# Routing a mixture of experts on one core: the outputs of 20 tiles go through memory and come back as one row per token

## The reference

```python
gates = sinkhorn(gate_logits)                    # 8 iterations; [b, token, expert], 8 experts
g = jnp.swapaxes(gates, -1, -2)
gv, idx = jax.lax.top_k(g, m)                    # each expert takes m = 64 of 512 tokens
hard_gates = (gate_values > 0.5).astype(x.dtype)
routed = xh[bi, hi, routed_indices]
out = jnp.einsum('bhmei,ehio->bhmeo', routed, experts4)
out = out * hard_gates[..., None]
y = jnp.zeros_like(xh).at[bi, hi, routed_indices].set(out)   # the last write of a token wins
x = x + y
```

## Time and profile before

| | |
|---|---|
| median of 3 runs | 493.18 us (491.93 to 494.08) |
| profiled execution, its own time | 492.21 us |
| span of its profile | 490.5 us |
| busy share of the span | PE 85%, DVE 82%, ACT 63%, POOL 47% |
| attention and its preparation | 0 to about 375 us |
| Sinkhorn | to 418.4 us |
| top 64 | 418.4 to 436.2 us |
| ranks | 437.3 to 449.3 us |
| weights and bits | 449.3 to 453.5 us |
| selection | 453.5 to 487.8 us |
| last output DMA | 487.8 to 490.5 us |

### The profile page before, as it was taken

How to read it: one execution, slowest core, us unless ns; L and a number is a source line. 1 busy time by engine, 2 the same in 40 slices (tenths; PEclk the granted TensorE clock), 3 DMA queues, 4 the chain that set the end, 5 groups by cost and what they waited for, 6 DMA issues and landing times.

```text
span 490.5 us, 9349 instructions
## 1 busy us (share of the span) xinstructions
PE 418.8 (85%) x2827; PEld 209.1 (43%) x2827; DVE 404.0 (82%) x1616; ACT 308.9 (63%) x599; POOL 228.1 (47%) x411
## 2 busy tenths in 40 slices
PE   5448987998999999899999989999988965999563
PEld 4233444464545546344554644555444432434121
DVE  6968756898898789788878978887986876996997
ACT  1002684788678769867876986887777432543871
POOL 3142573567466356746635674543433210000895
PEclk9955988999999999999999999999999999999998
DMA  8770143035027004402701440270001010100122
GB/s 261 213 174 2 49 135 76 34 115 113 21 78 182 25 33 131 99 20 77 182 25 45 126 110 2 97 162 24 2 1 64 2 43 0 43 23 21 43 65 86
DMA packets 28434, 36.85 MB, mean 75 GB/s; under 512 B 2144, under 2 KB 24224, under 8 KB 26912
## 3 DMA queue, kind: packets, MB, share of 16 engines
q1 hardware_dynamic: 27312, 34.68, 25.4%
q10 hardware_dynamic: 1072, 1.57, 1.3%
HBM read 19.41 MB, written 16.78 MB: 74 GB/s over the span
## 4 chain that ended last, share of the span: by engine, by line
PE 53%; DVE 23%; ACT 8%; issue 7%; DMA 5%; POOL 1%; SPq 1%; POOLq 1%; DVEq 1%; ACTq 0%
PE PVB L494 11%; PE ROWB L469 10%; PE CHB L482 9%; PE MB L526 6%; PE MB L502 4%; PE MB L536 4%; ACT YS L736 4%; DVE JUNK L938 3%; DMA YS<-parts_scratch 3%; PE ROWB L628 3%; DVE YS L1229 2%; PE CHB L628 2%; DVE CHB L1229 2%; PE MB L515 2%; DVE X L1235 2%
## 5 line engine op out<-in xcount | busy, mean ns | idle before, releaser
L938 DVE CUSTOM_DVE_ANT_0 JUNK<-ROWB,TRI 128x384 bf16<-128x384 f32 (+3 forms) x512 | 221.7, 485 | 41.7 <-PE ROWB L469 38.2
L736 ACT ACTIVATE YS<-CHB 128x512 f32<-128x512 f32 x320 | 172.9, 612 | 44.0 <-PE CHB L482 43.7
L858 POOL TENSOR_SCALAR_AFFINE_SELECT YS<-YS 128x256 f32<-128x256 f32 x256 | 102.4, 410 | 147.2 <-ACT YS L736 139.4
L469 PE MATMUL ROWB<-YS 96*128 96x384 bf16 (+3 forms) x512 | 122.2, 312 | 13.1 <-DVE MX L938 7.1
L482 PE MATMUL CHB<-YS 104*128 104x384 bf16 (+3 forms) x512 | 116.4, 303 | 7.4 <-ACT YS L736 5.0
L494 PE MATMUL PVB<-YS,VP 128*32 128x512 f32 (+3 forms) x1024 | 95.2, 446 | 5.1 <-POOL YS L858 5.1
L469 PEld LDWEIGHTS ROWB<-YS 96*128 96x128 bf16 x512 | 43.8, 100 | 89.9 <-DVE MX L938 47.1
L696 ACT ACTIVATE YS<-MB 8x1024 bf16<-8x1024 bf16 x32 | 32.5, 1017 | 57.4 <-PE MB L515 57.4
L482 PEld LDWEIGHTS CHB<-YS 104*128 104x128 bf16 x512 | 46.0, 98 | 41.7 <-ACT YS L736 17.6
L494 PEld LDWEIGHTS PVB<-YS,VP 128*32 128x32 f32 x1024 | 35.1, 109 | 31.7 <-POOL YS L858 17.5
L938 DVE DVE_READ_ACCUMULATOR2_ANT MX<- 128x1 f32 x512 | 42.2, 82 | 0.0
(11 more groups left out here) (131 smaller groups left out, 520.0 us busy)
## 6 DMA issues: line engine op xcount, KB each, us to landing
YS<-parts_scratch SPq DMA_DIRECT2D x28, 384.0 KB, 6.7
parts_scratch<-PARTS SPq DMA_DIRECT2D x15, 384.0 KB, 2.4
parts_scratch<-PARTS SPq DMA_DIRECT2D x15, 256.0 KB, 2.1
X<-in_x SPq DMA_DIRECT2D x8, 256.0 KB, 5.4
xn_scratch<-XN2S SPq DMA_DIRECT2D x8, 256.0 KB, 2.0
XS<-xn_scratch SPq DMA_DIRECT2D x8, 256.0 KB, 2.6
out<-X SPq DMA_DIRECT2D x8, 256.0 KB, 2.3
parts_scratch<-PARTS SPq DMA_DIRECT2D x15, 128.0 KB, 1.7
```

The lines of the kernel that those rows point to most:

```text
L469: last = pe.matmul(ROWP[BANK[u]][:, col:col + keys], QP[par][0:ROWS_K, pair, P * qb:keys], KZ[par][i % 2][0:ROWS_K, pair, 0:keys], start=T ...
L736: act.activation(PT[s % 2][:, c, :], CH[BANK[c]], ACT.Exp).then_inc(exp_done, 1)
L858: pool.affine_select(out=v, in_=v, pattern=[[0, 2], [1, P]], compare_op=ALU.is_ge, fill=0.0, base=0, channel_multiplier=-1).then_inc(causa ...
L938: last = dve.tensor_tensor_reduce(out=JUNK[BANK[u]][:, col:col + n], in0=ROWP[BANK[u]][:, col:col + n], in1=TRI[:, T - n:T], scale=1.0, sc ...
```

## The change

- The outputs of tiles 0 to 19 still go to `YS`, and SP stores each from there to a memory tensor `expert_outputs` (512 KB a tile; one row of 128 values for each token and expert, row 0 all zeros). The loads of `XS` for batches 2 to 6 stand between these stores in SP's program.
- ACT's scaling, POOL's sums and the DVE steps on stored tiles are gone. DVE works out a row number for each token of the 20 tiles (`IDX`, 0 if the token gets nothing). POOL then issues 20 indirect DMAs; each reads one row for each of 128 tokens and adds it to `X`.
- DVE selects only tiles 20 to 31, in six pairs, both of a pair from PSUM. A fourth bank pair (`ROWP[2]`, `MB`) is added; PE's tile 24 and later wait for the pair before last.
- Ranks: for each pair of lists PE now makes four small products, with 128 columns of `OH` as the weights and two columns of `RANKC` moving. They land with tokens on partitions, so the copy to `RT` and the four transposes go. The half tiles stand after pairs 6, 12, 18 and 24.
- The first round of the top 64 reads PSUM; the copy to `GT` goes. So does the copy of `BITS` to PSUM.
- The outputs of batches 5 to 7 are issued by ACT, those of 0 to 4 by SP.
- `SMALL` grows by 160 columns (80 KB); POOL clears one more row (`NOTHING`) at the start.

The diff, without declarations and without the host's table:

```diff
@@ -127,28 +127,20 @@
 DIRECT = 5
 STORED = DIRECT * TB
-SHARE = [[2, 3]] * DIRECT
-OTHERS = [[t for t in range(TB) if t not in own] for own in SHARE]
+ROWS_AT = T + 2 * B * E - 2 + E
-OWN = [(b, t) for b in range(DIRECT) for t in SHARE[b]]
-PAIRED = [((n // TB, n % TB), OWN[n - STORED]) for n in range(STORED, B * TB - 2)] + \
-         [((B - 1, TB - 2), (B - 1, TB - 1))]
+PAIRED = [((n // TB, n % TB), ((n + 1) // TB, (n + 1) % TB)) for n in range(STORED, B * TB, 2)]
 SELECT_STEPS = 4
 def selected_by(b):
     return 2 * SELECT_STEPS * (1 + max(k for k, pair in enumerate(PAIRED) if any(of == b for of, _ in pair)))
-def folded_by(b):
-    return 4 * sum(map(len, OTHERS[:b + 1]))
 class Batch:
...
@@ -274,10 +264,11 @@
         SUMS = (ROWP[2], MB)
         FIRSTB = ROWP + CH[0:2]
         EXPB = [CHB[:, 0:2 * T], ROWB[:, 0:2 * T]]
-        DIRECTB = [(CH[0], CH[1]), (ROWP[0], ROWP[1]), (CH[2], PVB[:, :])]
-        BITP = ROWP[2][:, 0:3 * B * TB].rearrange("p (k n) -> p k n", k=3)
+        DIRECTB = [(CH[0], CH[1]), (ROWP[0], ROWP[1]), (CH[2], PVB[:, :]), (ROWP[2], MB[:, :])]
+        y_dram = nc.dram_tensor("expert_outputs", [1 + STORED * P * E, C], F32, kind="Internal").ap()
         xn2_dram = nc.dram_tensor("xn2_scratch", [B, P, T], F32, kind="Internal").ap()
         scratch = nc.dram_tensor("parts_scratch", [2, 2, PRODUCTS, HD, 2, PAIRS, T], BF16, kind="Internal").ap()
...
@@ -432,15 +413,19 @@
             load_xn2(0)
             load_xn2(1)
             save_xn2(B - 1)
-            for b in range(2, B):
+            sp.dma_start(y_dram[0:1, :], NOTHING[:, :]).then_inc(y_saved, 16)
+            for n in range(STORED):
+                sp.wait_ge(y_copied, n + 1)
+                sp.dma_start(y_dram[1 + P * E * n:1 + P * E * (n + 1), :].rearrange("(p e) c -> p (e c)", e=E),
+                             YS[:, C * E * n:C * E * n + C * E]).then_inc(y_saved, 16)
+                if n % TB == TB - 1:
+                    load_xn2(n // TB + 2)
+            for b in range(DIRECT + 2, B):
                 sp.wait_ge(y_full, TB * (b - 1))
-                if b == B - 1:
-                    sp.wait_ge(xn2_saved, 16 * B)
+                sp.wait_ge(xn2_saved, 16 * B)
                 load_xn2(b)
-            for b in sorted(range(B), key=lambda b: (selected_by(b), -b)):
-                sp.wait_ge(chain, selected_by(b))
-                if b < DIRECT:
-                    sp.wait_ge(folded, folded_by(b))
+            for b in range(DIRECT):
+                sp.wait_ge(gathered[b], 16 * TB)
                 sp.dma_start(out[b].rearrange("(t p) c -> p t c", p=P), X[:, TB * b:TB * b + TB, :]).then_inc(out_saved, 16)
             sp.wait_ge(out_saved, 16 * B)
...
@@ -623,8 +608,10 @@
                     pe.wait_ge(xs_ready[b % 2], 16 * (b // 2 + 1))
                     if 2 <= n < STORED + 2:
                         pe.wait_ge(y_copied, n - 1)
-                    elif n >= STORED + 3:
-                        pe.wait_ge(chain, 2 * SELECT_STEPS * (n - STORED - 2))
+                    elif n == STORED + 3:
+                        pe.wait_ge(w_ready, 1)
+                    elif n >= STORED + 4:
+                        pe.wait_ge(chain, 2 * SELECT_STEPS * ((n - STORED) // 2 - 1))
                 last = pe.matmul(buffer(n, half), XS[b % 2][:, P * t:P * t + P],
                                  WEXP[:, 4 * half:4 * half + 4, :].rearrange("p e o -> p (e o)"),
                                  start=True, stop=True)
@@ -678,14 +665,12 @@
             for j in range(B * E // 2):
                 pe.wait_ge(onehot, j + 1)
-                last = pe.matmul(ROWP[2][0:B * E, :], RANKC[:, MID - 2 * j:MID - 2 * j + B * E], OH[j % 8][:, :],
-                                 start=(j == 0), stop=(j == B * E // 2 - 1)).then_inc(onehot_used, 1)
-                if j % 8 == 7:
+                for t in range(TB):
+                    last = pe.matmul(MB[:, B * E * t + 2 * j:B * E * t + 2 * j + 2], OH[j % 8][:, P * t:P * t + P],
+                                     RANKC[:, MID:MID + 2], start=True, stop=True)
+                last.then_inc(onehot_used, 1)
+                if j in (6, 12, 18, 24):
                     experts_next(1)
-            pe.wait_ge(rt_ready, 1)
-            for t in range(TB):
-                last = pe.transpose(MB[:, B * E * t:B * E * t + B * E], RT[:, P * t:P * t + P], IDF[0:B * E, 0:B * E])
-            last.then_inc(ranks_turned, 1)
             experts_next(2 * (B * TB - STORED))
@@ -794,20 +779,16 @@
             for n in range(DENSE_END - 1, STORED):
                 copy_outputs(n)
-            act.wait_ge(w_ready, 1)
-            order = [(b, t) for b in range(DIRECT) for t in OTHERS[b]]
-            for j, (b, t) in enumerate(order):
-                if j >= 2:
-                    act.wait_ge(folded, 4 * (j - 2) + 1)
-                for e in range(E):
-                    last = act.activation(WY[j % 2][:, e, :], outputs(TB * b + t, e), ACT.Copy, scale=weight(b, t, e))
-                last.then_inc(weighted, 1)
+            for b in range(DIRECT, B):
+                act.wait_ge(chain, selected_by(b))
+                act.dma_start(out[b].rearrange("(t p) c -> p t c", p=P), X[:, TB * b:TB * b + TB, :]).then_inc(out_saved, 16)
         @block.gpsimd
         def _(pool):
             pool.memset(NHALF[:, :], -0.5)
+            pool.memset(NOTHING[:, :], 0.0)
+            pool.drain()
             pool.memset(ONES[:, :], 1.0).then_inc(built, 1)
             def rstd(n, stats, mv, dst, shift, done):
@@ -890,17 +871,13 @@
             rstd(B, ln2_stats, MV2, RSTD2[:, :], SHIFT2[:, :], ln2_rstd)
-            order = [(b, t) for b in range(DIRECT) for t in OTHERS[b]]
-            for j, (b, t) in enumerate(order):
-                x = X[:, TB * b + t, :]
-                pool.wait_ge(weighted, j + 1)
-                pool.tensor_tensor(SUM4[:, :, :], WY[j % 2][:, 0:4, :], WY[j % 2][:, 4:8, :], ALU.add).then_inc(folded, 1)
-                pool.wait_ge(folded, 4 * j + 1)
-                pool.tensor_tensor(SUM2[:, :, :], SUM4[:, 0:2, :], SUM4[:, 2:4, :], ALU.add).then_inc(folded, 1)
-                pool.wait_ge(folded, 4 * j + 2)
-                pool.tensor_tensor(SUM1[:, :], SUM2[:, 0, :], SUM2[:, 1, :], ALU.add).then_inc(folded, 1)
-                pool.wait_ge(folded, 4 * j + 3)
-                pool.tensor_tensor(x, SUM1[:, :], x, ALU.add).then_inc(folded, 1)
+            pool.wait_ge(y_saved, 16 * (STORED + 1))
+            pool.wait_ge(index_ready, 1)
+            for b in range(DIRECT):
+                for t in range(TB):
+                    pool.indirect_dma_start(X[:, TB * b + t, :], None, y_dram[:, :],
+                                            bass.IndirectOffsetOnAxis(ap=IDX[:, t, b:b + 1], axis=0),
+                                            compute_op=ALU.add).then_inc(gathered[b], 16)
         @block.vector
@@ -1153,20 +1130,19 @@
             dve.wait_ge(gt_ready, 1)
-            dve.tensor_copy(GT[0][:, :], CH[2][0:B * E, :])
-            dve.drain()
             ROUNDS = TOPK // 8
             for r in range(ROUNDS):
+                values = GT[r % 2][:, :] if r > 0 else CH[2][0:B * E, :]
                 if r > 0:
                     dve.wait_ge(top_removed, r)
-                dve.max(out=TOPV[r % 2][:, :], in_=GT[r % 2][:, :]).then_inc(top_found, 1)
+                dve.max(out=TOPV[r % 2][:, :], in_=values).then_inc(top_found, 1)
                 dve.wait_ge(top_found, r + 1)
                 if r < ROUNDS - 1:
                     if r > 0:
                         dve.wait_ge(top_placed, r)
-                    dve.match_replace(out=GT[1 - r % 2][:, :], in_to_replace=TOPV[r % 2][:, :], in_values=GT[r % 2][:, :],
+                    dve.match_replace(out=GT[1 - r % 2][:, :], in_to_replace=TOPV[r % 2][:, :], in_values=values,
                                       imm_value=-1.0).then_inc(top_removed, 1)
-                dve.max_index(out=TOPI[:, 8 * r:8 * r + 8], in_max=TOPV[r % 2][:, :], in_values=GT[r % 2][:, :]
+                dve.max_index(out=TOPI[:, 8 * r:8 * r + 8], in_max=TOPV[r % 2][:, :], in_values=values
                               ).then_inc(top_placed, 1)
             dve.wait_ge(top_placed, ROUNDS)
             dve.tensor_copy(TOPF[:, 0, :], TOPI[:, :])
@@ -1185,10 +1161,8 @@
+            dve.tensor_scalar(OPEN[:, :, :], GATES[:, :, :, :].rearrange("p t b e -> p (t b) e"), 0.5, None, ALU.is_gt)
             dve.wait_ge(onehot_used, B * E // 2)
-            dve.tensor_copy(RT[:, :], ROWP[2][0:B * E, :]).then_inc(rt_ready, 1)
-            dve.tensor_scalar(OPEN[:, :, :], GATES[:, :, :, :].rearrange("p t b e -> p (t b) e"), 0.5, None, ALU.is_gt)
-            dve.wait_ge(ranks_turned, 1)
             numbers = SMALL[:, T + 2 * B * E - 2:T + 2 * B * E - 2 + E].unsqueeze(1).to_broadcast([P, TB * B, E])
             dve.scalar_tensor_tensor(out=KEY[:, :, :], in0=MB[:, 0:TB * B * E].rearrange("p (t e) -> p t e", e=E),
```

(40 more changed lines are left out.)

19 lines of the change are left out of this document (9 added, 10 removed).

## The result

| | before | after |
|---|---|---|
| median | 492.3 us (490.5 to 494.1, 14 runs) | 495.7 us (493.6 to 498.2, 14 runs) |
| profiled execution, its own time | 492.21 us | 498.22 us |
| span of its profile | 490.5 us | 496.0 us |

These are runs of both kernels side by side. The ratio is 1.007, with an interval of 1.005 to 1.009: slower by 0.7%, 3.4 us. The forecast was 484.1 us, faster. The range (479 to 496) held the time by 0.3 us, and the case that came was rival (d). The profiled execution is the slowest of the fourteen. It lies 2.5 us over the median; 1.1 us of that stands in the trace before the change is reached (the first batch's attention result is added to `X` at 109.2 us, in the trace of before at 108.0), and the ten tiles of top 64 end 1.6 us later than there (437.87 against 436.23).

The account below looks back on a forecast made before the run. The chain that ended last was taken as the bound: PE, then DVE's weights and selection. Afterwards POOL ends last: 454.4 + 22.0, landing 2.3, output 2.74, span 481.4, median 484.1 us; range 479 to 496.

Parts of the forecast that it names:

- rival (d): Selection's end: gathers over 1.56 us make the change lose; held until rows land, 2.3 us each, time 508; chance 0.15.
- POOL's way: Selection's end: POOL starts at 454.4, issues 20 gathers of 1.1 us, ends last; span 481.4 us.
- The sum's own rule: Whole span: 459.4 us plus 20 times the price of a gather, if that is over 477.3.
- The tail: After the last gather: 2.3 us for its landing, then 2.74 us for the output of batch 4.
- break-even price of 1.56: POOL's gathers: at 1.56 us each the span equals the old 490.5 us; above it the change loses.
- The bounds, 0.32 and 2.6: Price of one gather on POOL: at least SP's 0.32 us per issue, at most 2.6 us, its whole way.
- PE's and DVE's way: Selection of tiles 20 to 31: PE sets the pace, DVE done at 474.5, span 477.3 if last.
- The ranks: Rank stage before `KEY`: small products at 0.07 us, 9.0 us in all, half tiles 4.2; +0.8 us.
- The clock: Warning that PE's granted clock might fall during two-column products; tiles of 3.4 us would push DVE's end to 488.
- Weights: DVE steps before selection: three more of 0.4 us, +1.2 us; the dropped copy of `BITS`, -0.3 us.
- The stores: Stores sharing SP's queue with `XS` loads in top 64: 0 cost, or 2 us at 200 GB/s.
- The start: Kernel start: `SMALL` larger by 80 KB, 0.3 us later; POOL's extra clearing, 0.

Follow-up runs that it names:

- e2: The changed kernel with each gather adding only 64 bytes of a row instead of 512, still 128 rows; one execution took 496.3 us.
- e3: The changed kernel with each gather serving 64 rows instead of 128; one execution took 493.7 us.
- e6: The changed kernel with six of the 20 stored tiles selected by DVE from `YS`, leaving 14 gathers; 485.1 us, ratio 0.985 to the kernel before.
- e7: The changed kernel with 20 gathers that only copy into `YS`, and DVE adding the rows to `X` four tiles at a time; 491.7 us, ratio 1.001.
- e9: The changed kernel with only the addition taken from the gathers, so rows overwrite `X`; 486.9 us, ratio 0.988.
- e11: The kernel of e9 once more, unchanged, one traced execution; 484.8 us.
- e8: The kernel of e7 with four stored batches instead of five, so 16 copying gathers; 494.3 us, ratio 1.003.
- e1: The changed kernel with gathers that only copy their rows into `YS`, nothing added to `X`; one execution took 487.95 us.

## Why the prediction was wrong, point by point

- **POOL's way: the step that failed.** The mechanism was right: POOL becomes the last, its DMAs start at 454.16 (forecast 454.4), they stand one behind the other, and the batch that ends last is SP's. The term 20 x 1.1 us was mis-sized: it measured 20 x 1.85. The sum's own rule gives 459.4 + 20 x 1.85 = 496.4 us, and the span is 496.0. The tail holds too: from the end of the last gather 2.36 us to its landing (3.9 less 1.54; forecast 2.3) and 2.5 to write out (2.74). The whole miss of 14.6 us in the span is 15.0 from this term, less 0.4.
- **So close a fit is in part luck.** This is the slowest of the fourteen executions; by the medians the miss is 11.6 us. And the start of the row at 454.16 comes from errors that cancel: the stage of the ranks begins 1.6 us later than in the trace of before (forecast 0.3), the ranks take 1.4 us less (forecast 0.8 more), and POOL takes 0.82 us to start (forecast 0.1). In the traces of e2 and e3, with the same work before the gathers, the row starts at 452.5 and 452.6.
- **How 1.1 was chosen.** The nearest row was taken to be a POOL instruction that runs software, 1.05 us. For a gather without the addition that is fair: 0.94 in the instruction. It missed two things. The 0.30 us between two gathers was in no row of that kind; and the addition was costed at nothing, as part of the transfer. It costs POOL 0.60 us. The break-even price of 1.56 had been worked out, and it lies between the two kinds of gather (1.25 and 1.85). The bounds, 0.32 and 2.6, were right and left nearly all of the answer open. With one step of the sum unpriced, 20 times in a row, at the end of the chain, and with the break-even well inside its bounds, 0.74 for "faster" was more than these rows could carry.
- **Rival (d)** was given 0.15, with a way to it that isn't the one found: a gather doesn't hold POOL until its rows have landed. POOL is free after 1.54 us, the landing is at 3.9. The Trainium skill (DMA: Bandwidth & Descriptors, Anatomy of one DMA) has about 2.0 us of fixed cost for a DMA. Nothing like it adds up: 1.25 or 1.85 us is the spacing, and the page's 1 us to the first byte (Specifications) is another thing than POOL's time: no view here has the first byte, and the page says nothing of 0.60 us for the addition.
- **PE's and DVE's way: right.** DVE ends at 473.55 (forecast 474.5), and it waits about half a microsecond for PE in each of pairs three to six. With POOL out of the way the change would have ended near 476.3 (473.55 + 2.74, an estimate that no run tested); e6 has a span of 484.4 with 14 gathers.
- **The ranks: wrong in sign.** Forecast +0.8 us; from the transposition of the indices to `KEY` it is 12.1 us (437.87 to 449.98) instead of 13.5 (436.23 to 449.76). A product with its weight load is 0.025 us (28 of them in 0.69) and not 0.07. Up to the first half tile the stage runs at the pace of DVE's one-hot tiles (15 in 4.03 us), and PE takes the four products of each as it comes. From there on PE is the chain: its four half tiles take 6.65 us (1.89, 1.92, 1.87 and 0.97) where the forecast had 4.2, and DVE waits for it three times, 1.9 us together. So the cheap products gained more than the sign tells, and the clock took part of it back. In e7, e9 and e11 the granted clock over the stage is 0.84 and not 0.72, and from the start of `IT` to `KEY` it takes 10.5 us instead of 11.9. The 81 ns that the Trainium skill (TensorE: Matmul & The Clock Gate, Back-to-back issue gap) gives for a load and product of 128 columns are for a moving operand of 128 columns and not of two, as the page has it, and the rate seen here is three times that.
- **The clock.** The warning came true in the ranks: the granted clock is 0.72 there, and half tiles take 1.9 us instead of 0.97. By 447.5 it is back, and through the selection it is 1.00, so the 3.4 us per tile that was feared didn't come (it did in e8, behind PE's pause). It was low in Sinkhorn too, 0.74 from 405 to 412 us where before has 1.00, in this trace and in most of the others, but not in e7 and e11, which have the change as well. No run shows why.
- **Weights: right.** `PICK`, `IDXF` and `IDX` start 0.40 us apart, and the row numbers are ready 1.5 us after `W` begins; POOL then takes 0.82 us to start, which the forecast had not, and an earlier `KEY` made up for it.
- **The stores: right.** In top 64 each tile still takes PE 1.72 us and none waits for `XS`, whose loads land after 3.5 us there instead of 2.6, while the core's DMAs move 305 GB/s in that window, more than the 263 the forecast allowed itself.
- **The start: not tested.** In the traces of all thirteen kernels and repeats the first batch's result stands at 107.5 to 109.2 us, the small table's two at 108.0 and 108.6. The 0.3 us can't be seen in this.

## What to carry to other kernels

Work moved off busy engines is worth nothing if its replacement ends later than they did. A chain of DMA issues on one engine is such a replacement: count them, and if their price is unknown, let the price at which the change loses set its chance. Then balance by number, not by kind: 20, 16 and 14 gathers gave 1.007, 0.991 and 0.985 of the time before. And let a faster variant be judged by its timeline, since a disturbance can hide in the slack of one kernel (e9) and cost the next one its gain (e8).

## What the runs showed of the hardware that was not expected

- POOL is held 0.94 us by an indirect DMA of 128 rows, and 1.54 us by one that adds (the first of a row 1.23 and 1.80), with 0.30 us between two. Rows of 64 and of 512 bytes cost it the same; 64 rows instead of 128 save 0.13 us.
- A gather that adds puts 2880 packets for 20 tiles on the queue, one that copies 640. The copying ones land later all the same (5.1 us against 3.9, in e1, the one such trace that has landings), and in most of their traces the DMA engines are busier.
- Weight loads of 128 columns with products of two columns follow each other every 0.025 us where their operands are ready, and TensorE's granted clock is 0.84 or less over the stage filled with them, in every trace that has it; in the kernel before it is 1.00.
- Beside copying gathers 1.25 us apart, tiles that PE has finished by its record reach DVE up to 10 us late (in e9 the last tile ends at 468.7 and is taken up at 479.26). The cause was not found.
